# A four-layer graph network on one core: layer 2's loop over edges with streamed one-hots, its bias multiplied into PSUM, and 1/deviation by Newton steps on VectorE

## The reference, cut to what matters

```python
x = x + L0(relu(layernorm(x)));  x = x + L1(relu(layernorm(x)));  f = relu(layernorm(x))
# layer 2, for all edges at once
src_h = f @ W_src + b_src;   dst_h = f @ W_dst + b_dst
se = src_h[src];             de = dst_h[dst]
h    = gelu(se @ W1a + de @ W1b + b1)
h    = gelu(h @ W2 + b2)
msg  = layernorm(h @ W3 + b3, ln_g, ln_b)        # (h - mean) * rsqrt(var + 1e-5) * g + b
gate = sigmoid(gelu(se @ Wg1a + de @ Wg1b + bg1) @ Wg2 + bg2)
upd  = segment_sum(gate * msg, dst)
x = x + upd @ W_out + b_out;  x = x + L3(relu(layernorm(x)))
```

## Time and profile before

| what | before |
|---|---|
| median of 3 runs | 13543.78 us (13542.45 to 13545.95) |
| the profiled execution's own time | 13554.67 us |
| its span, first to last instruction | 13552.9 us |
| busy: TensorE, VectorE, ScalarE, GpSimd | 64%, 62%, 35%, 67% of the span |
| TensorE's mean granted clock | 0.703 of full speed |

### The profile page before, as it was taken

The page is one execution under the profiler, slowest core; times in us unless marked ns, Lnnn a source line. Parts: engine busy times, 40 slices in busy tenths (PEclk is TensorE's granted clock), DMA queues, the critical chain, the costliest instruction groups (busy, mean ns, idle before and its releaser), DMA issues. The chain is left out here.

```text
span 13552.9 us, 205844 instructions
## 1 busy us (share of the span) xinstructions
PE 8663.9 (64%) x47919; PEld 6761.7 (50%) x47920; DVE 8457.2 (62%) x30343; ACT 4762.8 (35%) x13637; POOL 9123.7 (67%) x9335
## 2 busy tenths in 40 slices
PE   3310273777788867776555355558888677767776
PEld 0000132676677756776444255557777444444444
DVE  9960132777644457876444522248888688877887
ACT  0000162444333324552000111126555456645654
POOL 5777777766566647776777377727777377746775
PEclk9999965777655557775555566779999866665565
DMA  0000152222455552224555344432222444454445
GB/s 16 2 2 18 44 210 63 52 50 50 69 118 118 118 87 52 53 53 74 130 129 129 62 132 131 131 73 82 78 79 78 73 126 131 129 99 132 129 131 104
DMA packets 633653, 1199.12 MB, mean 88 GB/s; under 512 B 208682, under 2 KB 319944, under 8 KB 632136
## 3 DMA queue, kind: packets, MB, share of 16 engines
q0 software_dynamic: 305600, 572.24, 22.9%
q1 hardware_dynamic: 327560, 622.33, 13.9%
HBM read 960.69 MB, written 233.16 MB: 88 GB/s over the span
## 5 line engine op out<-in xcount | busy, mean ns | idle before, releaser
L432 POOL DMA_INDIRECT WK<-tab,IDX x4640 | 4467.8, 963 | 1969.1 <-issue 1287.1
L1227 POOL DMA_INDIRECT B<-tab,IDX x1856 | 1761.3, 949 | 950.3 <-issue 500.8
L755 PE MATMUL PS<-WK 128*128 128x129 f32 x5568 | 1172.7, 375 | 643.6 <-ACT WK L973 487.1
L755 PEld LDWEIGHTS PS<-WK 128*128 128x128 f32 x5568 | 998.3, 269 | 847.1 <-ACT WK L973 403.0
L1357 ACT ACTIVATE B<-B 128x33 f32<-128x33 f32 x5568 | 1211.1, 308 | 24.5
L1246 DVE TENSOR_REDUCE WK<-PS 128x1024 f32 (+1 forms) x928 | 1131.1, 1220 | 135.4 <-PE PS L1372 128.5
L432 POOL DMA_INDIRECT H<-tab,IDX x928 | 902.4, 972 | 347.0 <-issue 256.7
L342 POOL DMA_INDIRECT recd<-B x831 | 818.7, 985 | 338.9 <-issue 271.4
L342 POOL DMA_INDIRECT recd<-REC,B x831 | 837.9, 1008 | 272.5 <-issue 272.5
L1405 PEld LDWEIGHTS PS<-B,H 128*128 128x128 f32 x3712 | 815.5, 328 | 274.1 <-DVE ACC L1259 236.0
L718 PE MATMUL PS<-WK,B 128*128 128x2 f32 x3712 | 603.4, 284 | 544.2 <-DVE WK L631 543.0
(11 more groups left out here) (383 smaller groups left out, 20014.1 us busy)
## 6 DMA issues: line engine op xcount, KB each, us to landing
H<-onehots SPq DMA_DIRECT2D x232, 768.0 KB
onehots<-B SPq DMA_DIRECT2D x232, 384.0 KB
B<-onehots SPq DMA_DIRECT2D x232, 384.0 KB
WK<-onehots SPq DMA_DIRECT2D x232, 384.0 KB
WK<-tab,IDX POOLq DMA_INDIRECT x4640
onehots<-WK SPq DMA_DIRECT2D x232, 256.0 KB
onehots<-B SPq DMA_DIRECT2D x232, 128.0 KB
B<-tab,IDX POOLq DMA_INDIRECT x1856
```

The lines of the kernel that those rows point to most:

```text
L432: po.indirect_dma_start(out=G[:, g % n, k, :], out_offset=None, in_=table, in_offset=bass.IndirectOffsetOnAxis(ap=IDX[:, idx, t:t + 1], ax ...
L755: mm = pe.matmul(AG(r, k // 2), OH[:, r, k, :], R[:, r % 2, k, 0:129], start=k % 2 == 0, stop=k % 2 == 1)
L1227: po.indirect_dma_start(out=eG[:, g % 4, k, :], out_offset=None, in_=tab[TW3], in_offset=bass.IndirectOffsetOnAxis(ap=IDX[:, o, t:t + 1], ...
```

## The change

Layer 2's loop (stage d) is rewritten on all five engines:

- The one-hots are not made, transposed and copied from PSUM any more. They are read from DRAM, where layer 0 has left them: a new `d_sp` issues two transfers a turn, the transposed ones in bfloat16 (128 KB, which ScalarE converts to `dOT`) and the plain ones (256 KB, `dOH`, now a ring of four).
- b3, split in three bfloat16 parts, is multiplied by a matrix of ones into PSUM, and W3's products are added on top of it; the result stays in PSUM, bank 4 or 7 by turns (`Z3`), where VectorE takes its statistics and ScalarE reads it for r.
- The gate's multiply and reduce become four `scalar_tensor_tensor` with `accum_out`.
- The power on GpSimd becomes a guess by integer arithmetic and three Newton steps on VectorE, once for two groups, in turns in which j - 6 is odd: 16 small instructions of 8 columns a partition, of which 13 wait for the one before.
- The order of blocks and lags changes: TensorE's turn is now q2 (lag 5), ag (9), sv (2), p3 (6), zt (4); ScalarE's is r (8), tanh (6), copy (1), h1 (4), h2 (5); VectorE's last step, the add to `ACC`, has lag 10.

```diff
         def d_po(po, p):
             at, ring = raised_before(p)
             meet(po)
-            for j in range(NG + 6):
-                if j >= 6:
-                    g = j - 6
-                    po.wait_ge(S.mv, at.mv + g + 1)
-                    po.wait_ge(S.r, at.r + g - 1)
-                    po.tensor_tensor(dRS[:, g % 2, :], dVE[:, g % 2, :], dPW, ALU.pow).then_inc(S.rs, 1)
+            for g in range(NG):
+                po.wait_ge(S.z, at.z + g - 3)
+                rows_po(po, p, 0, tab[256], dG, g)
...
+        def d_sp(sp, p):
+            at, ring = raised_before(p)
+            for j in range(NG + 5):
                 if j < NG:
-                    po.wait_ge(S.z, at.z + j - 3)
-                    rows_po(po, p, 0, tab[256], dG, j)
+                    sp.wait_ge(S.ot, at.ot + j - 3)
+                    sp.dma_start(dSTt[:, j % 4, :], oht[0][j, :, 0:256].bitcast(BF16)).then_inc(s_kd[j % 4], 16)
+                if j >= 5:
+                    g = j - 5
+                    sp.wait_ge(S.ag, at.ag + g - 3)
+                    sp.dma_start(dOH[:, g % 4, :, :].rearrange("p k n -> p (k n)"),
+                                 oht[0][g, :, 256:768]).then_inc(s_st[g % 4], 16)
...
-                if x := turn(j, u, 9):
+                if x := turn(j, u, 10):
                     add_ve(ve, at, 0, *x, AGd)
...
+                if x := turn(j, u, 5):
+                    g, r = x
+                    ve.wait_ge(S.h1, at.h1 + g + 1)
+                    ve.wait_ge(S.th, at.th + g - 1)
+                    ve.wait_ge(S.gl, at.gl + g)
                     for k in range(4):
-                        i = ve.bn_stats(dBN[:, qz, k, :], dZ3[:, qz, 128 * k:128 * k + 128])
+                        i = ve.scalar_tensor_tensor(dGP[:, k, :], dGG[:, r % 2, 128 * k:128 * k + 128], 1.0, dWG, ALU.mult,
+                                                    ALU.mult, accum_out=dGL[:, r % 2, k:k + 1])
+                    i.then_inc(S.gl, 1)
+                if x := turn(j, u, 6):
+                    g, r = x
+                    ve.wait_ge(S.p3, at.p3 + g + 1)
+                    ve.wait_ge(S.mm, at.mm + g - 1)
+                    for k in range(4):
+                        i = ve.bn_stats(dBN[:, r % 2, k, :], Z3(r)[:, 128 * k:128 * k + 128])
                     i.then_inc(S.bn, 1)
...
+                    ve.wait_ge(S.bn, at.bn + g + 1)
+                    ve.wait_ge(S.rs, at.rs + g - 2 - r % 2)
+                if y := turn(j, u, 8):
+                    gy, ry = y
+                    ve.wait_ge(S.rs, at.rs + gy + 2 - ry % 2)
+                    ve.wait_ge(S.ag, at.ag + gy - 1)
+                    ve.tensor_copy(dR[:, ry % 2, :, 128], dGT[:, ry % 4, :]).then_inc(S.gw, 1)
+                if x:
                     for k in range(4):
-                        i = ve.bn_aggr(dMV[:, qz, k, :], dBN[:, qz, k, :])
+                        i = ve.bn_aggr(dMV[:, r % 4, k, :], dBN[:, r % 2, k, :])
                     i.then_inc(S.mm, 1)
...
+                    if r % 2 == 1:
+
+                        c = slice(r % 4 - 1, r % 4 + 1)
+                        ve.wait_ge(S.mm, at.mm + g + 1)
+                        ve.wait_ge(S.th, at.th + g + 1)
+                        ve.wait_ge(S.r, at.r + g - 3)
+                        ve.wait_ge(S.gw, at.gw + g - 3)
+                        ve.tensor_scalar(dGT[:, c, :], dTH[:, c, :], 0.5, 0.5, ALU.mult, ALU.add)
+                        ve.tensor_scalar(dV, dMV[:, c, :, 1], EPS, None, ALU.add).then_inc(S.nw, 2)
+                        ve.wait_ge(S.nw, step(g, 1))
+                        ve.tensor_scalar(dHV, dV, -0.5, None, ALU.mult).then_inc(S.nw, 2)
+                        ve.tensor_scalar(dT.bitcast(I32), dV.bitcast(I32), 1, None, ALU.arith_shift_right).then_inc(S.nw, 2)
+                        ve.wait_ge(S.nw, step(g, 3))
+                        ve.tensor_scalar(dY.bitcast(I32), dT.bitcast(I32), -1.0, float(MAGIC), ALU.mult, ALU.add).then_inc(S.nw, 2)
+                        for n in (4, 7, 10):
+                            ve.wait_ge(S.nw, step(g, n))
+                            ve.tensor_tensor(dT, dY, dY, ALU.mult).then_inc(S.nw, 2)
+                            ve.wait_ge(S.nw, step(g, n + 1))
+                            ve.tensor_tensor(dT, dT, dHV, ALU.mult).then_inc(S.nw, 2)
+                            ve.wait_ge(S.nw, step(g, n + 2))
+                            ve.scalar_tensor_tensor(dY, dT, 1.5, dY, ALU.add, ALU.mult).then_inc(S.nw, 2)
+                        ve.wait_ge(S.nw, step(g, 13))
+                        ve.tensor_tensor(dGW[:, c, :], dGT[:, c, :], dY, ALU.mult).then_inc(S.nw, 2)
+                        ve.wait_ge(S.nw, step(g, 14))
+                        ve.scalar_tensor_tensor(dNM[:, c, :], dMV[:, c, :, 0], -1.0, dGW[:, c, :], ALU.mult,
+                                                ALU.mult).then_inc(S.rs, 2)
...
             def body(j, u):
+                if f := turn(j, u, 8):
+                    g, r = f
+                    q = r % 2
+                    ac.wait_ge(S.rs, at.rs + g + 2 - r % 2)
+                    ac.wait_ge(S.ag, at.ag + g - 1)
+                    for k in range(4):
+                        i = ac.activation(dR[:, q, k, 0:128], Z3(r)[:, 128 * k:128 * k + 128], ACT.Identity,
+                                          bias=dNM[:, r % 4, k:k + 1], scale=dGW[:, r % 4, k:k + 1])
+                    i.then_inc(S.r, 1)
...
+                if f := turn(j, u, 1):
+                    g, r = f
+                    streamed(ac, p, g, r)
+                    ac.wait_ge(S.sv, at.sv + g - 1)
+                    ac.activation(dOT[:, r % 2, :], dSTt[:, r % 4, :], ACT.Copy).then_inc(S.ot, 1)
...
-                if f := turn(j, u, 1):
-                    turned_ac(ac, at, *f, dOT, 0)
...
+                if f := turn(j, u, 5):
+                    g, r = f
+                    ac.wait_ge(S.q2, at.q2 + g + 1)
+                    ac.wait_ge(S.p3, at.p3 + g)
+                    ac.activation(dH2, PS[:, 5, :], ACT.Gelu, bias=b2c).then_inc(S.h2, 1)
...
         def d_pe(pe, p):
             at, ring = raised_before(p)
 
             def body(j, u):
-                if f := turn(j, u, 6):
-                    g, r = f
-                    pe.wait_ge(S.h2, at.h2 + g + 1)
-                    for k in range(4):
-                        mm = pe.matmul(PS[:, 5, 128 * k:128 * k + 128], dH2[:, 128 * k:128 * k + 128], W3, start=True,
-                                       stop=True)
-                    mm.then_inc(S.p3, 1)
-                if f := turn(j, u, 1):
-                    turn_pe(pe, at, *f, dOH, 0, 1)
-                if f := turn(j, u, 8):
-                    sum_pe(pe, at, *f, dOH, dR, AGd, 1)
                 if f := turn(j, u, 5):
...
                     pe.wait_ge(S.h1, at.h1 + g + 1)
-                    pe.wait_ge(S.z3, at.z3 + g)
+                    pe.wait_ge(S.h2, at.h2 + g)
                     pe.matmul(PS[:, 5, :], W2, dHG[:, r % 2, 0:512], start=True, stop=True).then_inc(S.q2, 1)
-                if f := turn(j, u, 4):
-                    g, r = f
-                    pe.wait_ge(S.z, at.z + g + 1)
-                    pe.wait_ge(S.h1, at.h1 + g)
-                    for k in range(4):
-                        t = pe.transpose(PS[:, 3, 128 * k:128 * k + 128], dZ[:, r % 2, 256 * k:256 * k + 128], ident[:, :])
-                    t.then_inc(S.zt, 1)
+                if f := turn(j, u, 9):
+                    g, r = f
+                    landed_oh(pe, g, r)
+                    pe.wait_ge(S.gw, at.gw + g + 1)
+                    sum_pe(pe, at, g, r, dOH, dR, AGd, 1)
                 if f := turn(j, u, 2):
...
+                if f := turn(j, u, 6):
+                    g, r = f
+                    pe.wait_ge(S.h2, at.h2 + g + 1)
+                    pe.wait_ge(S.r, at.r + g - 1)
+                    pe.matmul(Z3(r), ONE3, B3P, start=True, stop=False)
+                    for k in range(4):
+                        mm = pe.matmul(Z3(r)[:, 128 * k:128 * k + 128], dH2[:, 128 * k:128 * k + 128], W3, start=False,
+                                       stop=k == 3)
+                    mm.then_inc(S.p3, 1)
+                if f := turn(j, u, 4):
+                    g, r = f
+                    pe.wait_ge(S.z, at.z + g + 1)
+                    pe.wait_ge(S.h1, at.h1 + g)
+                    for k in range(4):
+                        t = pe.transpose(PS[:, 3, 128 * k:128 * k + 128], dZ[:, r % 2, 256 * k:256 * k + 128], ident[:, :])
+                    t.then_inc(S.zt, 1)
             meet(pe)
-            sweep(pe, 8, body)
```

More of the change, by code:

```diff
@@ L754, in sum_pe @@
             for k in range(4):
-                mm = pe.matmul(AG(r, k // 2), OH[:, r, k, :], R[:, r % 2, k, 0:129], start=k % 2 == 0, stop=k % 2 == 1)
+                mm = pe.matmul(AG(r, k // 2), OH[:, r % OH.shape[1], k, :], R[:, r % 2, k, 0:129], start=k % 2 == 0,
+                               stop=k % 2 == 1)
             mm.then_inc(S.ag, 1)
```

(21 more changed lines are left out.)

92 lines of the change are left out of this document (26 added, 66 removed).

## The result

The changed kernel takes 14,541.76 us (median of 4 executions, 14,535.76 to 14,545.96), the kernel before, timed beside it, 13,544.87 us. The ratio is 1.073, with an interval of 1.0715 to 1.0752: slower by 997 us. The forecast was 14,390 us in a range of 13,990 to 14,850.

A forecast was written before the change was run, and what follows sets the result against it. VectorE and GpSimd were taken to set the pace of layer 2's stage, TensorE close behind. TensorE's 7.3 us, Newton to 8.5, loop ends to 9.0, clock to 10.3: 232 x (10.3 - 6.67) = 842 us, plus 3; 14,390 us, range 13,990 to 14,850.

The forecast's parts named there:

- The chain zt, h1, h2, q2: TensorE in layer 2's loop: q2 directly behind zt waits for ScalarE's GELUs, 1.85 us in each turn.
- TensorE's own 5.45 us: TensorE's work in a turn at the higher clock: q2, ag, sv, p3, zt and ones; with the wait 7.3 us.
- The ones: TensorE's multiply of 512 columns with the ones for b3: between 0.2 and 1.1 us, taken as 0.3.
- Newton's steps: VectorE, every second turn: 3.0 us, delaying ag and sv; sv 2.4 us later, 1.2 a turn, making 8.5 us.
- The clock: TensorE: stalls leave 3.5 us of each turn at 1.2 GHz, adding 1.3 us a turn, 9.0 to 10.3.
- Loop ends: Stall where the hardware loop of 8 turns comes round: 0.5 us a turn, 8.5 to 9.0.
- Costed at nothing: ScalarE's other work, one-hot transfers and gathers, SyncE's waits, GpSimd's 4.9 us: all fit inside the turn, no cost.
- (a): Rival: TensorE's clock stays up, 9.0 us a turn, 14,085 us; chance 0.21.
- (b): Rival: TensorE's clock stays down throughout, 13.25 us a turn, 15,070 us; chance 0.08.
- (c): Rival: Newton cheap or beside TensorE's wait, and the clock stays: 7.8 us a turn, 13,810 us; chance 0.08.
- (d): Rival, faster: the engines' sums decide, 6.2 us a turn, 13,430 us; chance 0.06.

The follow-up runs named there:

- e1: The changed kernel with TensorE's zt moved ahead of ag, directly behind q2 of the group before: stage 2495.3 us, 10.80 a turn, ratio 1.0485.
- e7: The changed kernel with TensorE's order made ones, p3, ag, q2, zt, sv: stage 2079.9 us, 9.00 a turn, ratio 1.0286.
- e5: The changed kernel with TensorE's stalls filled by matmuls that nobody reads, behind zt and ahead of ag: stage 2354.0 us, 10.19 a turn, ratio 1.0472.
- e4: The changed kernel without the three Newton iterations, 9 of 16 instructions, only the first guess kept: stage 2251.4 us, 9.75 a turn, ratio 1.0334.
- e6a: The kernel before with only layer 2's one-hots streamed from DRAM: stage 1426.5 us, 6.18 a turn, ratio 0.9899.

## Why the prediction was right, and where it was not

**The stage and the sum.** The stage sets the difference: 953 of 981 us. The forecast of 10.3 us a turn was 0.5 low. Of the 152 us between 14,390 and 14,542 that makes 108; 29 lie behind the last z, where I had counted nothing, and the rest is the difference between the profiled executions and the medians. That it comes so near is partly luck: the wait for Newton was put 0.65 us a turn too low and the clock 0.45 too high.

**The chain zt, h1, h2, q2.** 1.85 us by the earlier trace rows; measured, 1.86 on the mean of 228 turns. TensorE's own 5.45 us and this wait were to be 7.3; the turn without Newton is 7.43 to 7.44 in half of all cases, 7.7 to 8.0 in the others. The ones, taken at 0.3, start 0.31 ahead of p3.

**The step that failed.** I wrote of this chain "This decides, I think", and took it as a term that stands by itself. The sum came out right and the reason was half of it: with that wait cut by 1 us (e1) the turn is just as long, since p3, statistics, adds, ag, sv and p3 make a circle of the same 7.4 us. I had followed TensorE's instructions in their order and never the way from p3 back to p3. What e7 shows to matter is where p3 stands: behind ag and sv, Newton's steps lie in that circle; first in the turn, and with the first circle gone as well, 448 us come back. p3 moved alone, with q2 left directly behind zt, was not run.

**Newton's steps.** The mechanism was as predicted: in every second turn ag waits for the adds, which VectorE has behind Newton's steps. The size was not. 3.85 us instead of 3.0, from 0.27 us between dependent steps where I took 0.20 from the earlier trace rows, and 0.80 us ahead of L742 where I took 0.22 from the earlier trace rows. The 0.20 was the shortest of three such distances in the same loop. The row behind those of the earlier trace rows:

```profile
6904.00 0.16 DVE L899 TENSOR_TENSOR WK<-WK 128x4 f32<-128x4 f32 x1
```

It waits for L896 and starts 0.27 us behind it (6903.73), which is the median of 140 such pairs; from L893 to L896 the median is 0.20. Of the 5.4 us by which the long turn exceeds the short one, 3.7 are this wait (q2 to ag takes 4.65 us instead of 0.93), where I had 2.4. The rest is the clock: ag and sv take 1.7 us more.

**The clock.** 1.3 us a turn forecast; 0.75 by e5, and 1.7 in two turns, 0.85, by the rows of ag and sv. I had given every turn 3.5 us at 1.2 GHz. In fact short turns stay at full speed: 1.87 us of idle time ahead of q2 leave it at 1.10 us. In every long turn between 9840 and 10,060 us the clock falls within the second stall, in the one shown at its very start, and mostly stays low for nearly 7 us. So it is not the length of the second stall that brings it down. The Trainium skill ("TensorE: Matmul & The Clock Gate", HAM oscillation) tells of a clock that falls after longer idle gaps than these. Another section of its page (A second HAM failure mode) has a kernel whose clock oscillates from micro-idles between groups of matmuls. In this trace each is true of one kind of turn: with the stall of 1.87 us alone the clock stays up, and with a second one close behind it oscillates, even where the second is 1.13 us long (e4). The granted clock of the stage, 0.82, lies in the forecast's 0.70 to 0.85.

**Loop ends.** 0.5 a turn forecast, about 0.6 measured. **VectorE** takes 13.4 us for two turns' work, the idle times ahead of L742 included, 6.7 a turn instead of 5.67: the difference is the length of its Newton part and those idle times. As a sum it set nothing, for VectorE still waits 4 us for p3 in the long turn; the Newton part counts by its place in the circle.

**Costed at nothing.** ScalarE, GpSimd and the transfers: right. GpSimd waits for z, the streamed one-hots hold up nothing and by e6a are a gain. That the b3 product and the accumulating gate cost what was predicted is read from rows only; neither was tried alone.

**The rivals.** (a) and (b), the clock wholly up or wholly down, are excluded by the windows. (c) needed a cheap Newton, and e4, which leaves most of it out, still takes 9.75 us a turn. (d), the sums, did not come true for the change; its 6.2 us a turn is what e6a reaches, the edit that takes work from VectorE and adds no wait.

**What stays open.** Why e7's turns are 8.5 to 9.0 us long is read from a few turns and not tried. A version that had the streamed one-hots, the b3 product and the gate but a reciprocal for each group was not run, nor e7 with the power in place of Newton's steps.

## What to carry to other kernels

Work that is done for two groups at once joins their chains: the first waits for the second, and if a buffer or an engine's queue stands behind it, every second turn becomes as long as the whole chain. Follow each result once round, from an instruction to its own next instance, through each engine's order and each buffer's count; do this for every circle, since taking the wait out of one of two equal circles gives next to nothing. When the engines are well filled, take the edit that only removes work (here the streamed one-hots, 1%), and let those that add a wait be timed apart from it.
